# Making v of two attentions by pairs of 64-row matmuls, one PSUM bank for each half of the pair

## The reference, cut to what matters

```
x = x + conv_block(group_norm(x))
t = tokens(x)
t = t + attn1(layer_norm(t))          # causal, weights Wq, Wk, Wv (64 x 64)
t = t + ffn_program(layer_norm(t))

def attn1(x):
    q, k, v = x @ Wq.T, x @ Wk.T, x @ Wv.T
    att = where(causal, q @ k.T * scale, -inf)
    return softmax(att) @ v

def step(h, p):                        # 33 steps
    op = argmax(h[0, 0, :19])
    y = softmax((h @ wq[op]) @ (h @ wk[op]).T * scale) @ (h @ wv[op]) @ wo[op]
    h = where(attn_mask[op], y, h)
    z = relu(h @ w1[op] + b1[op]) @ w2[op] + b2[op]
    h = where(ffn_mask[op], z, h)
```

## Time and profile before

| | |
|---|---|
| median of 3 runs | 708.53 us (707.62 to 711.39) |
| profiled execution, device time | 711.64 us |
| its span, first to last instruction | 709.8 us |
| mean granted PE clock | 0.961 of 2.4 GHz |
| PE busy | 618.5 us (87%) |
| DVE busy | 581.7 us (82%) |
| ACT busy | 415.2 us (59%) |
| POOL busy | 451.1 us (64%) |

### The profile page before, as it was taken

How to read it: one execution, slowest core, us unless ns; L and a number is a source line. 1 busy time by engine, 2 the same in 40 slices (tenths; PEclk the granted TensorE clock), 3 DMA queues, 4 the chain that set the end, 5 groups by cost and what they waited for, 6 DMA issues and landing times.

```text
span 709.8 us, 10911 instructions
## 1 busy us (share of the span) xinstructions
PE 618.5 (87%) x3732; PEld 267.0 (38%) x3732; DVE 581.7 (82%) x622; ACT 415.2 (59%) x643; POOL 451.1 (64%) x240
## 2 busy tenths in 40 slices
PE   8889879889877888988878887988979999999996
PEld 3323222222222212222222222345756446777771
DVE  5799999999999999999999999364365457788755
ACT  4878777668567566766774663353445525544441
POOL 7599999999999999999999999510000220000002
PEclk9989999999999999989999999999899999999999
DMA  3876679686666675666666763000000000000001
GB/s 104 220 267 211 230 227 291 226 259 226 232 232 253 211 250 211 236 217 210 234 233 222 234 241 115 1 1 0 3 5 8 1 20 1 1 2 1 2 2 65
DMA packets 32107, 101.20 MB, mean 143 GB/s; under 512 B 6821, under 2 KB 7342, under 8 KB 32046
## 3 DMA queue, kind: packets, MB, share of 16 engines
q1 hardware_dynamic: 30486, 99.42, 41.6%
q10 hardware_dynamic: 1240, 0.88, 0.4%
q0 software_dynamic: 320, 0.13, 0.1%
HBM read 94.64 MB, written 2.10 MB: 136 GB/s over the span
## 4 chain that ended last, share of the span: by engine, by line
PE 44%; DVE 23%; issue 19%; ACT 7%; POOL 5%; DMA 1%; DVEq 0%; ACTq 0%; POOLq 0%
DVE hh_all L1641 9%; DVE pb L1636 8%; PE py L279 7%; PE pb L242 6%; PE px L302 5%; PE py L816 5%; POOL hc L1956 4%; PE pb L1044 2%; PE py L1068 2%; PE px L845 2%; PE pb L804 2%; POOL dbu L1967 2%; PE px L292 1%; DVE dtu_all L1615 1%; PE px L763 1%
## 5 line engine op out<-in xcount | busy, mean ns | idle before, releaser
L1956 POOL TENSOR_TENSOR hc<-hh_all,cc 128x1024 f32<-128x1024 f32 x128 | 298.5, 2355 | 6.3 <-DVE hh_all L1641 4.6
L1641 DVE TENSOR_TENSOR_SCAN hh_all<-da,pb 128x1024 f32<-128x1024 f32 x80 | 182.9, 2286 | 3.4 <-ACT da L1324 0.4
L1970 POOL TENSOR_TENSOR yg<-w_xs 128x512 f32<-128x512 f32 x10 | 12.6, 1266 | 227.1 <-DVE w_xs L1783 132.7
L816 PE MATMUL py<-hc,w_cst 64*64 64x512 f32 x1024 | 148.2, 639 | 8.5 <-DVE yg L1652 8.5
L1967 POOL TENSOR_TENSOR dbu<-bb,dtu_all 128x1024 f32<-128x1024 f32 x48 | 113.2, 2358 | 5.0 <-DMA bb<-scr 5.0
L1641 DVE TENSOR_TENSOR_SCAN hh_all<-pb,dbu 128x1024 f32<-128x1024 f32 x48 | 108.9, 2269 | 2.0 <-DVE dtu_all L1615 1.7
L1636 DVE TENSOR_TENSOR pb<-pb,dtu_all 128x1024 f32<-128x1024 f32 x80 | 97.1, 1214 | 3.7 <-PE pb L804 1.2
L804 PE MATMUL pb<-bc,w_sel 128*128 128x512 bf16 x160 | 51.8, 408 | 53.1 <-DVE hh_all L1641 53.0
L1324 ACT ACTIVATE da<-dt_all,w_aneg 128x1024 f32<-128x1024 f32 x80 | 89.8, 1138 | 2.7 <-DVE dt_all L1622 1.8
L1324 ACT ACTIVATE pb<-dt_all,w_aneg 128x1024 f32<-128x1024 f32 x48 | 53.6, 1116 | 64.3 <-DVE hh_all L1641 63.8
L816 PEld LDWEIGHTS py<-hc,w_cst 64*64 64x64 f32 x1024 | 31.2, 136 | 80.9 <-issue 54.4
(11 more groups left out here) (326 smaller groups left out, 1020.0 us busy)
## 6 DMA issues: line engine op xcount, KB each, us to landing
cc<-scr SPq DMA_DIRECT2D x128, 512.0 KB, 4.3
bb<-scr SPq DMA_DIRECT2D x48, 512.0 KB, 5.0
w_xs<-w_xm SPq DMA_DIRECT2D x8, 256.0 KB, 6.5
w_xs<-hc SPq DMA_DIRECT2D x6, 256.0 KB, 3.8
scr<-bcf SPq DMA_DIRECT2D x8, 128.0 KB, 4.6
out<-yg SPq DMA_DIRECT2D x4, 256.0 KB, 2.6
w_xst<-in_x SPq DMA_DIRECT2D x1, 512.0 KB, 4.6
w_cst<-in_consts ACTq DMA_DIRECT2D x1, 404.0 KB, 5.0
```

The source lines that it names most:

```text
L816: last = nc.tensor.matmul(py[part(t), half(r)], ident[part(r), part(r)], hc[u % NHC][part(r), half(t)], start=(n == 0), stop=(n == NS - 1) ...
L1641: nc.vector.tensor_tensor_scan(hh[u % NHH][:, :], decay[:, :], drive[:, :], 0.0, ALU.mult, ALU.add).then_inc(scan_done, 1)
L1956: nc.gpsimd.tensor_tensor(hc[u % NHC][:, :], hh[u % NHH][:, :], cc[u % NCC][:, :], ALU.mult).then_inc(hc_done, 1)
```

## The change

Both functions now handle eight groups of tokens at a time, a half h of the attention. For each group they issue two matmuls: one for the upper image with channels 0 to 63 as contraction rows and the 64 x 64 weight as moving operand, and one for the lower image on rows 64 to 127. Results of the upper image go to one bank, those of the lower to the other. So m = 2h + r now means image r of half h; it used to mean groups 4m to 4m + 3 of both images. The copies have the same size as before and the same place in their engines' order; `values(m)` writes runs of 64 values with gaps of 64 between them in place of one run. The waits for free banks of the picked attention, one for each bank before, both stand ahead of the first matmul of a half. Each bank's semaphore is raised by its own last matmul, the second last and the last of the sixteen.

```
     def pe_project_v(self, pe, k, src, wv, quads):
-        for m in quads:
-            if m == 0:
-                pe.wait_ge(self.fold_dve, 5 * k + 4)
-            pe.wait_ge((self.v_dve, self.v_act)[m % 2], 2 * k + m // 2)
-            for j in range(4):
-                g = 4 * m + j
-                last = nc.tensor.matmul((self.ob, self.rb)[m % 2][:, j * 128:(j + 1) * 128],
-                                        src[:, g * 128:(g + 1) * 128], wv[:, :], start=True, stop=True)
-            last.then_inc(self.v_full, 1)
+        h = quads[0] // 2
+        if h == 0:
+            pe.wait_ge(self.fold_dve, 5 * k + 4)
+        pe.wait_ge(self.v_dve, 2 * k + h)
+        pe.wait_ge(self.v_act, 2 * k + h)
+        for j in range(8):
+            g = 8 * h + j
+            for r in range(2):
+                rows = slice(C * r, C * r + C)
+                last = nc.tensor.matmul((self.ob, self.rb)[r][:, C * j:C * j + C], src[rows, g * 128:(g + 1) * 128], wv[rows, rows],
+                                        start=True, stop=True)
+                if j == 7:
+                    last.then_inc(self.v_full, 1)
...
     def values(self, m):
-        return self.vv[:, 4 * m:4 * m + 4, :, :].rearrange("p g r c -> p (g r) c")
+        return self.vv[:, 8 * (m // 2):8 * (m // 2) + 8, m % 2, :]
...
-        def pe_v(pe, m):
-            pe.wait_ge(zq_done, 2 * (m // 2) + 2)
-            for j in range(4):
-                g = 4 * m + j
-                last = nc.tensor.matmul(v_at[m][:, j * 128:(j + 1) * 128], zq[:, g * 128:(g + 1) * 128], w["wv1"][:, :],
-                                        start=True, stop=True)
-            last.then_inc(at.v_full, 1)
+        def pe_v(pe, h):
+            pe.wait_ge(zq_done, 2 * h + 2)
+            for j in range(8):
+                g = 8 * h + j
+                for r in range(2):
+                    last = nc.tensor.matmul(v_at[2 * h + r][:, C * j:C * j + C], zq[part(r), g * 128:(g + 1) * 128], w["wv1"][part(r), part(r)],
+                                            start=True, stop=True)
+                    if j == 7:
+                        last.then_inc(at.v_full, 1)
...
-                    for m in (2, 3):
-                        pe_v(pe, m)
+                    pe_v(pe, 1)
```

More of the change, by code:

```diff
@@ L980, in pe_first_pair @@
                     pe_mid_again(pe, c)
-                if n == 13:
-                    pe_v(pe, c)
+                if n == 13 and c == 1:
+                    pe_v(pe, 0)
             if n == NS:
```

## The result

| | before | changed |
|---|---|---|
| median | 708.76 us (707.62 to 712.86, 8 runs) | 714.13 us (710.77 to 714.62, 8 runs) |
| ratio to before | | 1.0044, 95% interval 1.0023 to 1.0064 |
| profiled execution | 711.64 us | 714.36 us |
| span | 709.8 us | 712.6 us |

The change makes the kernel slower by 0.44%, 3.1 us by the ratio (1.6 to 4.5), a little under what the prediction called distinguishable. The bare medians lie 5.4 us apart and the means of the eight runs 4.0, both more than the ratio says. The forecast was +1.1 us: the direction held, and most of the local terms did, but not the size.

The account below looks back on a forecast made before the run. The prediction took the chain of waits as the bound, PE holding 44% and DVE 23%. Its terms, 0.88 + 0.21 = +1.09 us, put the median of 708.53 at 709.6 us, range 706.9 to 712.4.

Parts of the forecast that it names:

- what the prediction called distinguishable: Whole kernel: a difference under 0.5% (3.5 us) is about what a measurement can't tell from no change.
- The length of a block: Blocks of v on PE: loads cost by columns, so the length stays, 1.94 us against 1.95; 0.0.
- Rivals 1: Blocks of v: loads on 64 rows cost half, block 1.10 us; net -0.6 us, 707.9 us; chance 0.17.
- 2 (3.7): Blocks of v: loads of both halves run one after the other, block 3.72 us; +6.4 us, 714.9 us; chance 0.04.
- rival 3: Blocks of v: load, then matmul, within each half of rows, block 2.75 us; +3.5 us, 712.0 us; chance 0.08.
- Place A: Group 7, first attention: ACT's first bank fills later, so its copy, exp and PE's turn all shift; +0.88 us.
- the 1.1 of the places: The forecast's sum over group 7 and the picked attention: 0.88 + 0.21 = +1.09 us.
- Place B: Picked attention, group 0: DVE's copy comes later, so PE's second block of v waits; +0.21 us, bounds +0.11 and +0.34.
- Place C: End of the scan: ACT's copies end about 0.6 us later, hidden by ACT's idle 4.35 us; 0.
- Copies with gaps: ACT's and DVE's copies of v, writing runs of 64 values: no change from 0.60 and 0.69 us.
- the forecast's own range: Whole kernel's time if the forecast, chance 0.64, holds: 708.7 to 711 us.
- slower by over 0.5%: Whole kernel: chance 0.10 that the change makes it slower by more than 0.5%.

Follow-up runs that it names:

- the first attention alone: The kernel before with the changed matmuls of v, and the changed copies, in the first attention only: ratio 1.0058 to the kernel before.
- the later repetitions: The changed kernel timed twice more, unaltered, against the kernel before: ratios 1.0057 and 1.0059.

## Why the prediction was right in part

**The length of a block** (0.0): held, 2.00 us, and its reason held, tested from both sides (128 moving columns 2.00 us, 64 stationary ones 1.15). Rivals 1 (1.1 us), 2 (3.7) and 3 (2.7) are out by that alone. The time came near rival 3's 712.0, by another mechanism than rival 3's; the trace keeps them apart, since its block would have been 0.8 longer.

**Place A** (+0.88): the turn is 0.84 us later, and the profiles without loss of clock differ by 0.83 to 0.89 at the landmark. The term is right for what it names.

**The sentence that failed** stands there too: all of it "shifts by 0.88", with nothing else behind it. I priced the wait as a shift and forgot that it is idle time of PE, and that PE's clock can fall behind it; filling the idle time took 3.5 us off the changed kernel. The page showed the exposure: PE's clock fell now and then all through the kernel, and the profile of before had 0.50 right behind this place. The missing term is the difference in how much of the next 13 us run at 1.2 GHz: 0 to 3.8 us in one execution, some 2 to 3 us on the mean (the changed kernel's 3.1 to 4.2 us by its three ratios less the 1.1 of the places). The clock's own reading agrees: 0.0055 to 0.0068 less on the mean over the runs of the changed kernel and of the first attention alone, at 0.39 us for each 0.001, is 2.2 to 2.7 us.

**Place B** (+0.21, bounds 0.11 to 0.34): +0.3, by luck in part. DVE's maximum came 2.79 us later than before (595.71 against 592.92) where ACT's copy ahead of the blocks came 2.48 later (589.05 against 586.57). The wait stood where it was forecast, on DVE's copy, 0.17 us. But the prediction has the turn at its old start, and it came late by itself: 0.09 us between the matmuls of L177 and the block (1.91 against 1.82) and 0.15 between the block and the turn (1.94 against 1.79). Before, the block's first load ran 0.43 us ahead of its first matmul, at 586.79 beside 587.22; changed, both start at 589.80. Less than half of what PE is late there is the wait, and no term of the sum has the rest.

**Place C** (0): held for the scan. Its last scan instruction on DVE started at 441.0 to 444.7 us in the profiles, but 6.74 or 6.75 us behind the v block in all but one, with either block (in the profile with doubled moving columns, 6.28). What the clock did behind the block, above, the prediction didn't have.

**Copies with gaps**: 0.60 and 0.69 us, as before. Nothing.

**Chances.** The ratio puts the changed kernel at 711.6 us on the first median of before, inside the range; the later repetitions put it at 712.6 and 712.7, just outside 712.4, and the bare median of the changed kernel, 714.13, lies outside too. It also lies above the forecast's own range, which ended at 711. That the time fell inside the whole range is luck: its top was set by rival 3, whose mechanism did not occur. The 0.10 for slower by over 0.5% was too low, since the clock stood nowhere in the working.

## What to carry to other kernels

Splitting a matmul over two halves of the rows gained nothing here, where the stationary operand has 128 columns and the moving one 64 or 128: it leaves each load's columns, and those set the pace. Filling two banks in turn in place of one after the other delays the first consumer by half a block; look who waits for the first bank. And an added wait on PE can cost more than its length, by what the clock loses behind it: read the granted clock in the stretch that follows the idle time, in more than one profile, and try an order of copies that shortens the idle time, or work that fills it, before judging the matmuls.

## What the runs showed of the hardware

- The stretches at 1.2 GHz behind group 7 were 0, 3.4, 6.8 or 10.2 us long, in executions of kernels that differ little or not at all (the changed kernel: 10.2, 3.4 and 10.2). 10.2 us cost 3.8 us, 6.8 us cost 3.1, and 3.4 us cost 1.0.
- The clock fell before PE resumed in one execution and after it in others: 0.7 us ahead of the turn in the changed kernel's first profile (503.65 against 504.35), 0.7 behind the turn's start in its second, and 2.2 behind it in the kernel before (504.73 against 502.52).
- With 1.98 us of idle time after a block of full matmuls the two profiles had none; after a block of 64-column pairs all four had it; after pairs of 128 columns the one profile had 3.4 us, and after pairs with 64 stationary columns too. With 1.37 us after 64-column pairs the one profile had 3.4 us.
- Weight loads of the two halves of the rows ran side by side over a whole block: 32 loads of 64 rows by 128 columns took 1.86 us, as long as 16 loads of 128 rows.
- Between matmuls on 128 rows and a block of pairs on 64 rows some time was lost: 0.09 us ahead of the block and 0.15 behind it at the picked attention, where the first load of a full block had run 0.43 us ahead of its matmul.
